# A recommendation tower on one core: one gathered field moved from GpSimd to 128 register-addressed loads of SyncE

## The reference

```python
e = jnp.stack([tbl_0[ids[:, 0]], ..., tbl_49[ids[:, 49]]], axis=1)   # (512, 50, 16)
gram = jnp.einsum('bid,bjd->bij', e, e)
pairs = gram[:, _I_IDX, _J_IDX]                                      # i < j: 1225 columns
x = concat(pairs, dense_ctx)                                         # 1241 columns
h1 = relu(x @ W_top1 + b_top1)                                       # 512
h2 = relu(h1 @ W_top2 + b_top2)                                      # 256
y = h2 @ W_top3                                                      # one number per sample
```

## Time and profile before

| | us |
|---|---|
| median of three executions | 141.55 (140.92 to 142.31) |
| profiled execution, its own time | 141.35 |
| its span (first to last instruction) | 139.5 |
| PE busy | 113.0 (81%) |
| POOL busy | 92.2 (66%), 96 gathers |
| DVE busy | 87.7 (63%) |
| ACT busy | 70.7 (51%) |

### The profile page before, as it was taken

The page is one execution under the profiler, slowest core; times in us unless marked ns, Lnnn a source line. Parts: engine busy times, 40 slices in busy tenths (PEclk is TensorE's granted clock), DMA queues, the critical chain, the costliest instruction groups (busy, mean ns, idle before and its releaser), DMA issues.

```text
span 139.5 us, 3054 instructions
## 1 busy us (share of the span) xinstructions
PE 113.0 (81%) x1237; PEld 103.2 (74%) x1237; DVE 87.7 (63%) x155; ACT 70.7 (51%) x104; POOL 92.2 (66%) x100
## 2 busy tenths in 40 slices
PE   0299979047759999999998959999759839999990
PEld 0188877046748999998897949988759838999980
DVE  6729978993898997797989697036830224323211
ACT  7769999997596995014800262042420072424110
POOL 1877777787777777787777877778777777740000
PEclk9999999956999999999999997799999999999999
DMA  2986999950001000000000000000001000010000
GB/s 63 311 319 193 415 406 394 304 168 11 5 7 14 9 11 5 7 7 12 6 5 12 7 7 6 10 7 7 9 10 7 7 7 11 5 12 0 0 5 1
DMA packets 5648, 9.78 MB, mean 70 GB/s; under 512 B 2149, under 2 KB 4710, under 8 KB 5504
## 3 DMA queue, kind: packets, MB, share of 16 engines
q1 hardware_dynamic: 2562, 8.79, 17.5%
q0 software_dynamic: 3072, 0.79, 5.9%
HBM read 9.55 MB, written 0.03 MB: 69 GB/s over the span
## 4 chain that ended last, share of the span: by engine, by line
POOL 55%; issue 22%; PE 16%; DMA 2%; ACT 1%; DVE 1%; ACTq 0%; DVEq 0%
POOL moving L240 31%; POOL moving L245 24%; PE psm L727 4%; PE gram L720 3%; PE pt L791 3%; PE gram L727 2%; PE p L727 2%; DMA ids_sb<-in_ids 2%; PE gram L701 1%; ACT blocks L183 1%; PE pt L780 1%; DVE mcols L507 1%; DVE h2w L568 0%; DVE scols L647 0%; DVE z L194 0%
## 5 line engine op out<-in xcount | busy, mean ns | idle before, releaser
L240 POOL DMA_INDIRECT moving<-tbl,ids_sb x48 | 46.4, 968 | 17.0 <-issue 14.3
L245 POOL DMA_INDIRECT moving<-tbl,ids_sb x48 | 45.5, 949 | 14.6 <-issue 14.6
L686 PE MATMUL psm<-table,onehot 128*128 128x160 f32 x208 | 37.3, 325 | 10.6 <-DVE picked L475 10.3
L727 PE MATMUL p<-z,w_sb 128*128 128x128 f32 x312 | 40.9, 284 | 1.6 <-DVE z L194 1.6
L686 PEld LDWEIGHTS psm<-table,onehot 128*128 128x128 f32 x208 | 31.7, 204 | 13.3 <-DVE picked L475 12.5
L727 PEld LDWEIGHTS p<-z,w_sb 128*128 128x128 f32 x312 | 38.5, 199 | 2.6 <-ACT z L194 1.7
L475 DVE TENSOR_TENSOR picked<-psm,mask 128x480 f32<-128x480 f32 (+1 forms) x36 | 22.4, 635 | 7.5 <-PE psm L686 6.6
L464 DVE TENSOR_REDUCE fixed<-picked 128x48 f32<-128x480 f32 (+1 forms) x36 | 22.2, 625 | 0.5
L189 DVE COPY z<-gram 63x384 f32<-63x384 f32 (+1 forms) x18 | 9.3, 516 | 20.3 <-PE gram L701 10.7
L183 ACT COPY blocks<-mcols 32x384 f32<-32x384 f32 (+3 forms) x18 | 14.9, 826 | 9.2 <-DVE mcols L529 6.0
L189 ACT COPY z<-gram 63x384 f32<-63x384 f32 (+1 forms) x18 | 7.9, 436 | 22.0 <-PE gram L720 17.3
(11 more groups left out here) (47 smaller groups left out, 77.7 us busy)
## 6 DMA issues: line engine op xcount, KB each, us to landing
w_sb<-in_w SPq DMA_DIRECT2D x1, 3072.0 KB, 14.4
wide<-quotients SPq DMA_DIRECT2D x3, 832.0 KB, 6.7
moving<-tbl,ids_sb POOLq DMA_INDIRECT x96, 2.4
table<-in_small SPq DMA_DIRECT2D x1, 720.0 KB, 5.9
table<-in_small SPq DMA_DIRECT2D x1, 640.0 KB
w_sb<-in_w SPq DMA_DIRECT2D x1, 512.0 KB
table<-in_small SPq DMA_DIRECT2D x1, 480.0 KB, 4.1
table<-in_small SPq DMA_DIRECT2D x1, 240.0 KB, 2.8
```

The source lines that it names most:

```text
L240: nc.gpsimd.indirect_dma_start(moving[:, t, YS + n, 0:D], None, tables[n], bass.IndirectOffsetOnAxis(ap=ids_sb[:, t, NS + n:NS + n + 1], a ...
L245: nc.gpsimd.indirect_dma_start(moving[:, t, XS + n, 0:D], None, tables[HALF + n], bass.IndirectOffsetOnAxis(ap=ids_sb[:, t, NS + HALF + n: ...
L686: ins = nc.tensor.matmul(psm[:, m % 2, (f - a) * R * D:(f - a + 1) * R * D], onehot[:, t % 2, f, :], table[:, f, :], start=True, stop=True)
L727: return nc.tensor.matmul(hidden_sums(t, k), w1_sb[:, c, P * k:P * (k + 1)], z[:, t, c, :], start=first, stop=last)
```

## The change

- **Rows by SP.** POOL no longer gathers the last late field of tile 3 (95 gathers instead of 96). In its place SP reads the id of each of the 128 samples out of SBUF into a register and issues a DMA of one row of 64 bytes whose address comes from that register. 24 of these (`AHEAD`) stand ahead of SP's wait for the load of tile 3's `wide`, 104 behind it. `turn_late(3, CUT, YS)` on DVE waits for all 128.
- **First ids apart.** `ids` is laid out with the large fields' ids ahead of the small ones', and loaded by two DMAs: the 24 columns that POOL needs for tile 0, then the remaining 176. POOL waits for the first alone, and for the second ahead of tile 1. The identity matrix and the small constants come in one DMA (`consts`) instead of two.
- **One comparison.** The mask's ten comparisons are one `tensor_tensor` over 1040 elements, which also waits for `consts`.
- **Shares.** In tile 3, ACT spreads one quarter and DVE three; in the others two and two as before.
- **Orders.** The lists of steps of ACT, DVE and PE are other ones.

```diff
@@ sync
+            def load_rows(first, last):
+
+                for p in range(first, last):
+                    row = sp.value_load(large_ids[p:p + 1, TILES - 1, NL - 1:NL])
+                    sp.dma_start(moving[p:p + 1, TILES - 1, YS - 1, 0:D], tables[NL - 1][bass.ds(row, 1), :]
+                                 ).then_inc(rows_loaded, 16)
+
-            sp.dma_start(ids_sb[:], ids).then_inc(ids_loaded, 16)
+            sp.dma_start(ids_sb[:, 0:NL], ids[:, 0:NL]).then_inc(first_loaded, 16)
             sp.dma_start(ids_t_sb[:], ids_t).then_inc(ids_t_loaded, 16)
-            sp.dma_start(iota[:], iota_in).then_inc(consts_loaded, 16)
-            sp.dma_start(ident[:], ident_in).then_inc(consts_loaded, 16)
+            sp.dma_start(ids_sb[:, NL:], ids[:, NL:]).then_inc(ids_loaded, 16)
+            sp.dma_start(consts[:], consts_in).then_inc(consts_loaded, 16)
...
             sp.dma_start(w3_sb[:], w3.to_broadcast([P, H2])).then_inc(w2_loaded, 16)
+            sp.wait_ge(ids_loaded, 16)
+            load_rows(0, AHEAD)
             sp.wait_ge(onehot_ready, NBC + NWC)
             sp.dma_start(wide[:, 1, :], quotients[3:4].to_broadcast([P, NS * P])).then_inc(wide_loaded[3], 16)
+            load_rows(AHEAD, P)
@@ gpsimd
-            pool.wait_ge(ids_loaded, 16)
+            pool.wait_ge(first_loaded, 16)
             for t in range(TILES):
+                if t == 1:
+                    pool.wait_ge(ids_loaded, 16)
...
-                for n in range(HALF):
+                for n in range(HALF if t < TILES - 1 else HALF - 1):
@@ shares, used by both spreads on both engines
+        def share(t, side):
+
+            n = Q // 2 if t < TILES - 1 else 1
+            return range(n) if side == 0 else range(n, Q)
@@ vector
-            for r in range(R):
-                ins = nc.vector.tensor_scalar(mask[:, :, :, r], rem[:], float(r), None, ALU.is_equal)
-            step(ins)
+            dve.wait_ge(consts_loaded, 16)
+            step(nc.vector.tensor_tensor(mask[:].rearrange("p t s r -> p (t s) r"),
+                                         rem[:].rearrange("p t s -> p (t s)").unsqueeze(2).to_broadcast([P, TILES * NS, R]),
+                                         iota[:, 1:1 + R].unsqueeze(1).to_broadcast([P, TILES * NS, R]), ALU.is_equal))
...
                 if a:
-                    dve.wait_ge(tail_gathered, 16 * (b - a))
+                    dve.wait_ge(tail_gathered, 16 * (b - a - 1))
+                    dve.wait_ge(rows_loaded, 16 * P)
@@ tensor, the last stretch
             product_x(3, 0, CUT)
-            chunks(layer3, 2)
+            chunks(layer3, 5)
             second_bias(3)
-            chunks(layer3, 3)
             product_x(3, CUT, YS)
```

More of the change, by code:

```diff
@@ L58 @@
 NSC = -(-NS // SC)
+AHEAD = 24
 ROUND = 1.5 * 2 ** 23
@@ L66, in field_groups, with build_tower @@
     return [(a, min(a + size, NS)) for a in range(0, NS, size)]
-def build_tower(nc, quotients, ids, ids_t, extra, small, w1, w2, b2, w3, ident_in, iota_in, out, *tables):
+def build_tower(nc, quotients, ids, ids_t, extra, small, w1, w2, b2, w3, consts_in, out, *tables):
     f32 = mybir.dt.float32
@@ L317, in spread_mid @@
                 act.wait_ge(zeroed[t % 2], 2 - t % 2)
-                for q in range(2):
+                for q in share(t, 0):
                     diagonal(nc.scalar.copy, t, q, YS, MS).then_inc(mid_blocks[0], 1)
@@ L515, in spread_mid @@
                     dve.wait_ge(y_made, 2 * (t - 1))
-                for q in range(2, Q):
+                for q in share(t, 1):
                     diagonal(nc.vector.tensor_copy, t, q, YS, MS).then_inc(mid_blocks[1], 1)
@@ new lines, in _ @@
+            broadcast(3)
+            select(0, 2)
+            broadcast(4)
+            select(0, 3)
+            broadcast(5)
+            selections(0, 4, 6)
+            broadcast(6)
+            selections(0, 6, NSC)
+            selections(1, 0, 3)
+            product_y(0)
+            select(1, 3)
+            layer0 = first_layer(0)
+            chunks(layer0, 1)
+            selections(1, 4, 7)
+            chunks(layer0, 1)
+            select(1, 7)
+            chunks(layer0, 1)
+            select(1, 8)
@@ L819, in _ @@
+            product_x(0, 0, YS)
+            selections(2, 0, 2)
+            chunks(layer0, 2)
+            select(2, 2)
+            chunks(layer0, 2)
+            select(2, 3)
+            chunks(layer0, 1)
+            selections(2, 4, 6)
             chunks(layer0, 3)
-            for u in range(5, NSC):
-                select(2, u)
-                chunks(layer0, 1)
-            select(3, 0)
+            product_y(1)
+            selections(2, 6, 8)
             chunks(layer0, 1)
-            product_y(1)
@@ L837, in _ @@
+            select(3, 4)
+            product_x(1, 0, YS)
+            select(3, 5)
+            chunks(layer1, 1)
+            selections(3, 6, 8)
+            chunks(layer1, 4)
+            product_y(2)
             chunks(layer1, 1)
             select(3, 8)
-            chunks(layer1, 5)
-            product_y(2)
+            chunks(layer1, 2)
+            layer2 = first_layer(2)
+            chunks(layer2, 3)
             second_layer(1)
-            layer2 = first_layer(2)
-            chunks(layer2, 5)
+            chunks(layer2, 1)
```

216 lines of the change are left out of this document (110 added, 106 removed).

## The result

| | before | after |
|---|---|---|
| median of four executions each | 141.93 (140.92 to 142.51) | 160.13 (159.18 to 160.26) |
| profiled execution | 141.35, span 139.5 | 160.26, span 158.5 |
| mean granted clock of PE | 0.963 | 0.88 |

The account below looks back on a forecast made before the run. The end was taken as set by the landing of tile 3's mid fields, their preparation and some 25 us of PE; 0.4 + 0.8 + 0.7 = 1.9 us off gave 139.6 us, range 138.4 to 143.5.

Parts of the forecast that it names:

- part 6: Rows by SP: a row costs 0.7 us, so the last lands at 106, hidden with 19 us to spare.
- the point that decides: Cost of a row on SP, 0.85 us, up to which the last row still lands in time for 124.9.
- The first rival: A row on SP costs more than 0.85 us and DVE waits: 158 at 1.0 us; chance 0.18 for well above.
- Part 1: POOL's last late gather of tile 3 removed: worth 0 at the end, last late data 1.25 us earlier.
- Part 2: POOL's start: the first ids, loaded apart, land earlier and save 0.4 us, between 0.2 and 0.45.
- Part 3: POOL's second gather: one comparison instead of ten no longer holds it, saving 0.8 us, bounds 0 to 0.87.
- the third: The single comparison holds POOL too, or the early ids bring little: 140.3 to 140.6 us; chance 0.17.
- Part 4: Tile 3's mid fields, between transpose and `product_y(3)`: uneven ACT and DVE shares save 0.7 us, between 0.6 and 0.75.
- Part 5: New orders in tiles 2 and 3: cost 0; first late transpose at 117.1, range 0 to 0.4 us of loss.
- the sum of 1.9 us: Earlier start of `product_y(3)`: 0.4 from the ids, 0.8 from the comparison, 0.7 from the shares.
- its second term: The 0.8 us that the single comparison was to save at POOL's second gather.

## Why the prediction was wrong

**The step that failed is part 6**: the price of a row. I took 0.7 us: 0.44 for the DMA, and 0.25 for the register load with its operation, on the model of a handover of 0.20 between two engines. Measured, the DMA alone is a step of 0.30, so load and operation take 0.68, of which the load is 0.50; the row is 0.98 on average, above the 0.85 that was worked out as the point that decides. The choice within 0.44 to 1.8 was the error, not the bounds: nothing in the rows said that a load is like a handover, and the load stood 0.50 us on SP's queue each time. The nearer row was the DMA that reads, writes and signals in 1.7 us. The estimate worked out from the Trainium skill, page "DMA: Bandwidth & Descriptors", section "Latency and other measured facts" (a floor of about 600 ns for a load, 1.04 us a row), was the better one; the runs give 0.50 and 0.98.

**The first rival's size.** At 1.0 us a row it gave 158; by its own rule, 1.28 us for each 0.01 above 0.85, 0.98 gives 139.6 + 16.6 = 156.2. What the rule says of the wait held: the piece was transposed at 141.80, 16.9 behind the 124.9 at which it was due (SP's first load came at 14.9, 0.9 late, and the load for `wide` took 0.4 from it, but the last row landed in 1.1 us instead of 1.7). What it left out comes behind the wait: 3.3 us of half clock and 0.5 of output transfer. Added up afterwards from the measured pieces, 139.6 + 16.9 + 3.3 + 0.5 = 160.3, measured 160.26.

**Part 1** (the gather less is worth 0): right, as far as the times tell. 138.91 with 95 gathers, 138.95 with 96.

**Part 2** (0.4 us from the ids): right, 0.36 in the changed kernel, 0.50 without the rows; in the kernels that keep the single load of ids, on chips at 141, the first gather itself starts between 3.03 and 3.16.

**Part 3** (0.8 from one comparison): wrong in its cause. The second gather is free of it without the rows, as forecast (0.94); in the changed kernel it took 1.18, over the 1.1 that the prediction had named. But the third is held, to 0.8 us behind the comparison's end. With the ten comparisons left in, nothing is held. Of the rivals, the third was nearest: the single comparison holds POOL too. The page "SBUF — State Buffer", section "Who interferes with whom", of the Trainium skill has `tensor_tensor` with both inputs in SBUF collide with GpSimd's reads, and infers that descriptor generation is free of it. The hold of 0.5 us (1.43 against 0.94) agrees with a collision, as a gather reads its ids from `ids_sb`; whether its descriptor generation was held too no trace shows. Of `tensor_scalar` it says that they may take the shared ports: ten of them went with a held gather in before (1.81) and with none at the gather of 5.50 (0.96). Which ports were taken no trace shows.

**Part 4** (0.7 from the shares): right in direction. From mid transpose to `product_y(3)` 2.86 us in the changed kernel and 2.88 without the rows, against 3.46: 0.6, the lower end of its range; against the same kernel with even shares 0.59.

**Part 5** (orders cost 0, first late transpose at 117.1): right where nothing else disturbs: 117.16 with ten comparisons and filling. In the changed kernel it is at 119.73, since `last_layer(2)` ahead of it waits for a PE at half clock.

**What no part had**: the half clock on `product_y(3)`. The rows of before had PE idle 2.73 us there and then run 2.04 us for 64 matmuls, and I took it as given. The gain of the other parts is in the trace (1.60 us at that place without the rows) and 1.46 of it was given back in the next product. With the filling and ten comparisons, `product_y(3)` comes at 112.18 and the second late piece at 126.62; forecast were 112.1 and 126.7. So the sum of 1.9 us came out, but in another kernel than the changed one, and its second term for another reason, the earlier ids and not the comparison; that it agrees so closely is in part luck.

## What to carry to other kernels

A load into a register held SP's queue for about 0.5 us here, and nothing on that queue overlapped it; if an address must come from a register, load many at once, and count the whole step times the number of rows against the latest time at which the last one is due. When an operation has no row and a decision point lies inside its bounds, say that the sign is open, and lean to the row that does the same kind of thing rather than to the shortest one. A gain of 1 to 2 us in a span of 140 can be hidden by a single stretch of half clock after an idle time: read the clock of the stretch behind every idle time of PE, and try filling that idle time with matmuls whose result nobody reads before judging the rest.

## What the runs showed of the hardware that was not expected

- With one more input of 512 bytes, loaded by SP, the output of 2 KB lands 1.4 us after its issue in all 15 profiles that have it, in six of which nobody reads it; in the five without it (before and after among them) 2.1 to 2.9. Why is not known.
- A gather is held by ten `tensor_scalar` that begin 0.34 us after it (1.81 us, before) and not by ten that began 0.64 us ahead of it (0.96, at 5.50); behind a single `tensor_tensor` of 1.24 us that runs when the gather starts, the gather ends 0.81 to 0.82 us after it in each of the eight profiles that have one (1.42 to 1.64 us long).
- Whether the half clock falls on a given idle time differs from kernel to kernel with nearly the same rows there: 2.73 us of idling ahead of `product_y(3)` without it in before, 2.65 us with it (0.53) in the kernel without the rows. Idle time ahead of it is thus not all that decides.
